# Attention: three PSUM banks in a ring for keys and transposed maxima; values, fold and sums of a unit in one bank

## What is computed

```
q = (layernorm(x) @ Wq + bq)   -> (4, 16, 1024, 32)
k = (ctx @ Wk + bk)            -> (4, 16, 2048, 32)
v = (ctx @ Wv + bv)            -> (4, 16, 2048, 32)
attn = softmax(clip(q @ k^T / sqrt(32), -1e4, 1e4))
x = x + tanh(g_xattn) * ((attn @ v) @ Wo + bo)
x = x + tanh(g_ffn) * ffn(layernorm(x))       # ffn: 512 -> 2048 -> 512, silu
```

## Time and profile before

| what | value |
|---|---|
| median of three runs | 3423.44 us (3421.34 to 3423.89) |
| the profiled execution | 3422.4 us, its span 3420.6 us |
| PE matmul busy over the span | 94% |
| PE weight load, DVE, ACT, POOL busy | 55%, 59%, 47%, 56% |
| attention, first scores to last gather | 477 us to 2459 us of the span |

### The profile page before, as it was taken

How to read it: one execution, slowest core, us unless ns; L and a number is a source line. 1 busy time by engine, 2 the same in 40 slices (tenths; PEclk the granted TensorE clock), 3 DMA queues, 4 the chain that set the end, 5 groups by cost and what they waited for, 6 DMA issues and landing times. The chain is left out here.

```text
span 3420.6 us, 51826 instructions
## 1 busy us (share of the span) xinstructions
PE 3212.1 (94%) x15941; PEld 1871.3 (55%) x15941; DVE 2032.0 (59%) x2788; ACT 1603.2 (47%) x2847; POOL 1909.7 (56%) x897
## 2 busy tenths in 40 slices
PE   6799979999999999999999999999656699999999
PEld 5688844444444444444444444444244588888887
DVE  8766656666666666666666666666469433333332
ACT  2222226666666666666666666666522111111111
POOL 4666537777777777777777777777554000000000
PEclk9899979999999999999999999999978899999999
DMA  5566672212222122212222122221195100000000
GB/s 170 187 209 213 213 223 57 56 39 54 56 56 51 42 56 56 55 46 47 56 56 55 41 53 56 56 51 43 57 279 176 40 25 25 25 25 25 15 14 22
DMA packets 142086, 263.11 MB, mean 77 GB/s; under 512 B 16961, under 2 KB 57921, under 8 KB 134721
## 3 DMA queue, kind: packets, MB, share of 16 engines
q1 hardware_dynamic: 141344, 253.82, 26.1%
q10 hardware_dynamic: 672, 8.39, 0.8%
HBM read 168.84 MB, written 93.32 MB: 77 GB/s over the span
## 5 line engine op out<-in xcount | busy, mean ns | idle before, releaser
L852 DVE TENSOR_REDUCE at_half_max<-ps 128x1 f32<-128x1024 f32 x1024 | 1245.0, 1225 | 635.0 <-PE ps L671 623.3
L790 ACT ACTIVATE at_probT<-ps 128x512 f32<-128x512 f32 x2048 | 1113.2, 595 | 418.6 <-PE ps L688 364.4
L620 POOL TENSOR_TENSOR at_gp_sum<-at_gp_sum,at_probT 128x1024 f32<-128x1024 f32 x512 | 1218.3, 2380 | 42.4
L671 PE MATMUL ps<-at_k_stack,at_q_stack 96*128 96x512 f32 x2048 | 868.2, 425 | 19.8 <-DMA at_k_stack<-kT_hi 18.2
L688 PE MATMUL ps<-at_q_stack,at_k_stack 98*128 98x512 f32 x2048 | 876.8, 429 | 9.3 <-ACT at_probT L790 3.4
L671 PEld LDWEIGHTS ps<-at_k_stack,at_q_stack 96*128 96x128 f32 x2048 | 390.1, 191 | 392.9 <-DVE at_half_max L852 202.0
L688 PEld LDWEIGHTS ps<-at_q_stack,at_k_stack 98*128 98x128 f32 x2048 | 385.8, 189 | 351.2 <-ACT at_probT L790 319.1
L615 POOL TENSOR_TENSOR at_gp_sum<-at_probT 128x1024 f32<-128x1024 f32 x128 | 304.9, 2382 | 431.9 <-ACT at_probT L790 431.9
L725 PE MATMUL ps<-at_probT,at_v_head 128*32 128x512 f32 x4096 | 542.4, 601 | 0.9 <-ACT at_probT L790 0.9
L1361 ACT ACTIVATE ff_y<-ps,ff_b_t 128x512 f32<-128x512 f32 x128 | 88.2, 689 | 612.8 <-PE ps L1324 612.8
L1376 POOL TENSOR_TENSOR ff_x_in<-ff_x_in,ff_b_half 128x2048 f32<-128x2048 f32 x8 | 36.8, 4602 | 601.6 <-DVE ff_x_in L1398 601.6
(11 more groups left out here) (154 smaller groups left out, 3890.2 us busy)
## 6 DMA issues: line engine op xcount, KB each, us to landing
at_k_stack<-kT_hi SPq DMA_DIRECT2D x128, 256.0 KB, 4.9
kT_hi<-kv_k_hi SPq DMA_DIRECT2D x16, 1024.0 KB, 4.2
kT_lo<-kv_k_lo SPq DMA_DIRECT2D x16, 1024.0 KB, 6.5
v_heads<-kv_v_out SPq DMA_DIRECT2D x16, 1024.0 KB, 5.7
at_q_stack<-qT_hi SPq DMA_DIRECT2D x128, 128.0 KB, 3.3
at_k_stack<-kT_lo SPq DMA_DIRECT2D x64, 256.0 KB, 4.3
at_v_head<-v_heads SPq DMA_DIRECT2D x64, 256.0 KB, 5.0
kv_c_in<-in_ctx_dram SPq DMA_DIRECT2D x16, 768.0 KB, 7.1
```

Source lines behind the costliest of these rows:

```text
L620: pool.tensor_tensor(gp_sum[lane % 2][:, :, :], gp_sum[lane % 2][:, :, :], pairs[:, 2 * i + 2:2 * i + 4, :], ALU.add).then_inc(gp_added, 1)
L671: mm = pe.matmul(ps[:, n, :], q_stack[buf][0:PARTS, rows], k_stack[buf][0:PARTS, BANK * n:BANK * (n + 1)], start=True, stop=True)
L790: act.activation(probT[lane % 2][:, kv, :], src, ACT.Exp).then_inc(exp_done, 1)
L852: dve.tensor_reduce(dst, src, AX_X, ALU.max).then_inc(max_done, 1)
```

## The change

Banks 4, 5 and 6 become a ring of three for the keys' tiles and the transposed maxima: 17 users to a unit, the maxima between tiles 13 and 14. A tile now waits for the exp of the tile three users back. Values, fold and sums all use bank 7. To make that possible, the four value sets stand in two blocks of two sets, the fold is made with the first sums a slot later, and the last sums stand alone in the slot behind. Values of the next unit wait for the gather. The diff, cut to the path that runs:

```
-    TURN, KEYS, PV, FOLD = 5, 6, 7, 12
+    TURN, KEYS, PV, SUMS, FOLD = 5, 6, (9, 10), 11, 12
+    RING = 3
+    def key_bank(lane, kv):
+        return 4 + ((KVT + 1) * lane + kv + 1 + (kv >= KVT - 2)) % RING
+    def turn_bank(lane):
+        return 4 + ((KVT + 1) * lane - 2) % RING
 # PE: keys
-                need(pe, exp_done, KVT * unit + kv - 1)
+                if kv:
+                    need(pe, exp_done, KVT * unit + kv - 2 + (kv >= KVT - 2))
-                pe.matmul(ps[:, 4 + kv % 2, :],
+                pe.matmul(ps[:, key_bank(lane, kv), :],
 # PE: turn_maxima
-                need(pe, gather_done, unit - 1)
+                need(pe, exp_done, KVT * unit - 4)
-                        mm = pe.matmul(ps[0:2, 7, cols], neg_hi[:, t, :], ident_r[:, :],
+                        mm = pe.matmul(ps[0:2, bank, cols], neg_hi[:, t, :], ident_r[:, :],
 # PE: values
-                    need(pe, partial_done, unit)
+                    need(pe, gather_done, unit)
-                        mm = pe.matmul(ps[D * g:D * (g + 1), 6, :], v_head[buf][:, 4 * r + g, :],
+                        mm = pe.matmul(ps[D * g:D * (g + 1), 7, :], v_head[buf][:, 4 * r + g, :],
+            def fold_values(base, slot):
+                unit, lane, r = unit_at(base, slot, SUMS)
+                if unit is None or r:
+                    return
+                pe.wait_ge(partial_done, unit + 1)
+                pe.matmul(ps[0:D, 7, :], A["fold"][:, :], partial[:, :], start=True, stop=True)
                 for g in range(1, 4):
-                    pe.matmul(ps[D * g:D * (g + 1), 7, :], ones[:, :], probT[lane % 2][:, KVT - 5 + g, :],
-                              start=True, stop=False)
+                    mm = pe.matmul(ps[D * g:D * (g + 1), 7, :], ones[:, :], probT[lane % 2][:, KVT - 5 + g, :],
+                                   start=True, stop=False)
+                mm.then_inc(partial_read, 1)
 # PE: last_sums keeps the wait for gp_added and the three last matmuls with ones
 # PE: step
-                fold(base, slot)
-                for r in range(QT):
-                    values(base, slot, PV + r, (r,))
+                values(base, slot, PV[0], (0, 1))
+                values(base, slot, PV[1], (2, 3))
+                fold_values(base, slot)
                 last_sums(base, slot)
                 turn_maxima(base, slot)
 # ACT: copy_partial
-                need(act, fold_done, unit)
-                act.copy(partial[:, :], ps[:, 6, :]).then_inc(partial_done, 1)
+                need(act, partial_read, unit)
+                act.copy(partial[:, :], ps[:, 7, :]).then_inc(partial_done, 1)
```

More of the change, by code:

```diff
@@ L543, in attend @@
     assert SK == 4 * BANK and HALVES == 2 and KVT == 16
+    assert BODY * (KVT + 1) % RING == 0
+    def key_bank(lane, kv):
+        return 4 + ((KVT + 1) * lane + kv + 1 + (kv >= KVT - 2)) % RING
+    def turn_bank(lane):
+        return 4 + ((KVT + 1) * lane - 2) % RING
     def unit_at(base, slot, lag):
@@ L591, in attend @@
         partial_done = sem("partial_done")
+        partial_read = sem("partial_read")
         fold_done = sem("fold_done")
@@ L697, in turn_maxima @@
                 pe.wait_ge(split_done, 5 * (unit + 1))
-                need(pe, gather_done, unit - 1)
+                need(pe, exp_done, KVT * unit - 4)
+                bank = turn_bank(lane)
                 for t in range(QT):
@@ L704, in turn_maxima @@
                         for part in range(2):
-                            mm = pe.matmul(ps[:, 7, cols], wide[:, part, t, :], ident_r[:, :],
+                            mm = pe.matmul(ps[:, bank, cols], wide[:, part, t, :], ident_r[:, :],
                                            start=(part == 0), stop=(part == 1))
                     else:
-                        mm = pe.matmul(ps[0:2, 7, cols], neg_hi[:, t, :], ident_r[:, :],
+                        mm = pe.matmul(ps[0:2, bank, cols], neg_hi[:, t, :], ident_r[:, :],
                                        start=True, stop=True)
@@ L728, in values, with last_sums @@
                     mm.then_inc(pv_done, 1)
-            def last_sums(base, slot):
-                unit, lane, r = unit_at(base, slot, PV + QT - 1)
+            def fold_values(base, slot):
+                unit, lane, r = unit_at(base, slot, SUMS)
                 if unit is None or r:
                     return
-                need(pe, gather_done, unit)
+                pe.wait_ge(partial_done, unit + 1)
+                pe.matmul(ps[0:D, 7, :], A["fold"][:, :], partial[:, :], start=True, stop=True)
                 for g in range(1, 4):
-                    pe.matmul(ps[D * g:D * (g + 1), 7, :], ones[:, :], probT[lane % 2][:, KVT - 5 + g, :],
-                              start=True, stop=False)
-            def fold(base, slot):
+                    mm = pe.matmul(ps[D * g:D * (g + 1), 7, :], ones[:, :], probT[lane % 2][:, KVT - 5 + g, :],
+                                   start=True, stop=False)
+                mm.then_inc(partial_read, 1)
+            def last_sums(base, slot):
                 unit, lane, r = unit_at(base, slot, FOLD)
@@ L743, in fold @@
                     return
-                pe.wait_ge(partial_done, unit + 1)
                 pe.wait_ge(gp_added, GP_ADDS * (unit + 1))
-                pe.matmul(ps[0:D, 7, :], A["fold"][:, :], partial[:, :], start=True, stop=True)
                 for g, tile in ((1, probT[lane % 2][:, KVT - 1, :]), (2, gp_sum[lane % 2][:, 0, :]),
@@ L788, in exps @@
                     act.wait_ge(tile_done, KVT * unit + kv + 1)
-                    src = ps[:, 4 + kv % 2, :]
+                    src = ps[:, key_bank(lane, kv), :]
                 act.activation(probT[lane % 2][:, kv, :], src, ACT.Exp).then_inc(exp_done, 1)
@@ L798, in copy_maxima @@
                     need(act, shift_done, KVT * (unit - 1))
-                    act.copy(neg_rows[lane % 2][:, :], ps[:, 7, :]).then_inc(row_copied, 1)
+                    act.copy(neg_rows[lane % 2][:, :], ps[:, turn_bank(lane), :]).then_inc(row_copied, 1)
                 else:
@@ L802, in copy_maxima @@
                     act.activation(q_stack[lane // HALVES][PARTS:PARTS + 2, q:q + BANK],
-                                   ps[0:2, 7, :], ACT.Identity).then_inc(row_copied, 1)
+                                   ps[0:2, turn_bank(lane), :], ACT.Identity).then_inc(row_copied, 1)
             def copy_partial(base, slot):
-                unit, lane, r = unit_at(base, slot, PV + QT - 1)
+                unit, lane, r = unit_at(base, slot, PV[1])
                 if unit is None or r:
@@ L894, in shift @@
                 need(dve, exp_done, n - 1)
-                dve.tensor_scalar(shifted[kv % 2][:, :], ps[:, 4 + kv % 2, :],
+                dve.tensor_scalar(shifted[kv % 2][:, :], ps[:, key_bank(lane, kv), :],
                                   A["clip_high"][:, 0:1], A["clip_low"][:, 0:1], ALU.min, ALU.max) \
```

## The result

The changed kernel takes 3307.04 us (median of four runs, 3304.32 to 3308.43), against 3423.66 us before. The ratio is 0.966, with a 95% interval from 0.9643 to 0.9676. That is 116.6 us less, where 102 were forecast. A second measurement, beside other kernels, gave 3307.41 us.

What follows compares the result with a forecast made beforehand. The prediction took PE as the bound, with 1.06 us per unit of waits for exponentials; less 0.26 for a new wait, 0.80 over 127 units saves 102 us, giving 3321 us, range 3283 to 3360 (own range 3295 to 3341).

Steps and rivals of the forecast that it cites:

- R1: Rival: score maxima don't gate PE, DVE's chain running at 1.80 us or PE's order giving time; 3289 us, chance 0.18.
- Waits for the exponentials: PE in attention: keys' matmuls wait for ACT's exp once in each slot; all 1.06 us per unit go.
- Regrouping of the values: PE's 32-column blocks: same sets and still four blocks per unit, so two value sets per block cost 0.
- One bank for values, fold and sums, and the maxima in the ring: Bank 7 shared, maxima moved into the ring: no new waits on gather, `partial`, POOL or exp; cost 0.
- The second value block: PE, slot behind the transposed maxima: needs exp 15 but does not wait, with 0.12 us to spare, the thinnest place.
- The new wait: PE at scores 0 waits for DVE's half maxima: 0.20 us per unit, 0.55 at a loop pass's end, mean 0.26.
- The sum: Attention: 1.06 us of waits removed less 0.26 added gives 0.80 us per unit, 102 us over 127 units.
- R2: Rival: ACT stays late after long blocks and copies, leaving half the exp wait, 0.5 us per unit; 3385 us, chance 0.20.
- R3: Rival: the change does nothing, the third bank's tile waiting for something else at the same time; 3423 us, chance 0.03.
- R4: Rival: DVE's chain becomes the bound at the two short slots, delaying another 0.80 us per unit; 3474 us, chance 0.05.
- R5: Rival: PE's clock falls to the lower level for a tenth of a unit, adding 1.4 us; 3499 us, chance 0.02.

Runs made afterwards that it cites:

- the fourth experiment: Fold and all sums put in one block, against the changed kernel with DVE's small instructions one reduction later; 3310.5 us, ratio 0.967.

## Why the prediction was right, point by point

The time was forecast as 3321 us and is 3307. That alone proves little, since it lies about midway between the forecast and R1 (3289 us); the unit, 14.43 us, too lies midway between 14.56 and 14.30. The terms decide, and each can be read from the traces.

*Waits for the exponentials (1.06 us per unit, all go).* Right in kind: none is left, and with two banks they are all back. The size was read a little too small. The unit without waits, worked out as 14.30 us, is 14.16 in the two kernels that have none. The step that was mis-sized is the distance of 0.35 us from the last full-width start to the block. I took it for the plain price of the switch, but it falls when the waits go. That last matmul is a tile of the keys. In the kernel before, the view has its weight load released by the exp, only 0.09 us ahead of the matmul (1509.62):

```profile
1509.53 0.19 PEld L688 LDWEIGHTS ps<-at_q_stack,at_k_stack 98*128 98x128 f32 x1 [0.19 <-ACT at_probT L790]
```

Over the blocks from 1300 to 1420 us the distance is 0.344 us on average before and 0.344 with two banks and the new grouping, but 0.321 with the ring and 0.318 where no wait is left. Four times in a unit, 0.026 us are 0.10 of the 0.14. The price without waits was read off a slot that had them. How a late weight load lengthens the distance behind its matmul is not shown.

*Regrouping of the values, 0.* Right within 5 us: with two banks it costs 5 (2 to 8). The Trainium skill's rule that a switch of the tiling mode drains TensorE (TensorEngine Tiling (Array Packing), section Key Properties) fits the fourth experiment, in which one block fewer saved 0.31 us while the sets stayed six.

*One bank for values, fold and sums, and the maxima in the ring, 0.* Right: the values, the fold and the sums all start 0.31 to 0.33 us behind the last full-width matmul, and the transposes follow the value block without a gap.

*The second value block, 0.12 us to spare.* It held, with less. In the changed kernel it starts 0.32 us behind the last full-width matmul, as the other blocks do. The exp of tile 15 ends at 1503.99 + 0.59 = 1504.58 and the block stands at 1504.70; less the 0.05 us that the prediction allows from an exp's end, 0.07 are left.

*The new wait, 0.26 us per unit on average.* Right: 0.27 by the difference of the units. By its rows it is 0.235 in the ordinary unit (0.20 forecast) and 0.62 at the loop's end (0.55), 0.30 on average, a little more than the units show. That the rows exceed the forecast has mostly the same cause as above: the short slot is 3.04 to 3.05 us and not 3.08, so scores 0 would stand earlier and waits longer. (Where the prediction says two matmul pairs, its 2 x 0.235 are two matmuls, which is what the order has.)

*The sum.* 1.06 - 0.26 = 0.80 was forecast; (1.06 + 0.14) - 0.27 = 0.93 against 0.91 measured. The 0.02 are the difference between the one unit of 15.36 us that was taken apart and the mean of 15.34.

*The rivals.* R1 did not happen, and its reason (POOL slows DVE) fell; the wait it dispensed with is real and worth 34 us when removed. R2 did not happen: no wait for the exp is left in the middle of attention. R3, no change, did not: the ratio is 0.966. R4's place is right and its size is not: the chain gates, at 0.27 us instead of more than 0.80. R5 did not: the granted clock stayed 1.00, though three banks go round.

## What to carry to other kernels

When a bound engine is full by its busy time, take one repeating stretch apart by the starts of its instructions; a wait cost its length here and 0.10 us more for the late weight load behind it. After a wait is removed, lay out the other engines' chains over the shorter slots: the next gate was visible, with its place and size, in the trace of before. A small chain that gates can be moved behind the work that is waited for, which gave 34 us here, and even the order of two waits ahead of it can count (12 us here).

## What had not been expected of the hardware

- Inside the loop the order of two waits ahead of an instruction of DVE was worth 0.10 us: 1.36 against 1.26 us from a reduction's start to the next instruction, and 12 us of the whole. With the wait that ends last also standing last it was the shorter.
- With POOL's adds cut from 2.38 to 0.22 us, DVE's reductions and small instructions kept their durations (1.22 and 0.15 to 0.16 us). The two did not disturb each other here.
- A block of 32-column matmuls costs about 0.31 us beyond its passes. Two blocks of one set made into one block of two sets saved that much, and blocks of one set (0.99 to 1.00 us) and of two (1.85 to 1.86) took the same time whether they held values, the fold or sums.
